# Sums of the first expert layer in two buffers, even and odd experts, the odd one added to the loaded rows by a GpSimd transfer

## The reference, cut to what matters

```python
scores = (x_flat @ Wg.T).T                       # 8 experts x 4096 tokens
top_vals, token_idx = top_k(scores, 512)         # each expert takes 512 tokens
token_w = softmax(top_vals, axis=-1)
xg = x_flat[token_idx]
h = silu(xg @ W1.T) * (xg @ W3.T)                # per expert
y = (h @ W2.T) * token_w[..., None]
out = zeros_like(x_flat).at[token_idx.reshape(-1)].add(y.reshape(-1, c))
```

## Time and profile before

| | us |
|---|---|
| median of 3 timed runs | 701.61 (701.60 to 701.68) |
| the profiled execution, its own time | 703.21 |
| the profiled execution, span from first to last instruction | 701.4 |
| busy in the span: PE, DVE, ACT, POOL | 514.5, 421.7, 343.0, 310.7 |

### The profile page before, as it was taken

One profiled execution on the slowest core, in us unless ns is written; L12 is line 12 of the kernel. 1 busy time (PEld: TensorE's weight loads), 2 busy tenths in 40 slices (PEclk: granted clock), 3 DMA queues, 4 the chain that ended last, 5 costly groups with the idle time before them and its releaser, 6 DMA issues.

```text
span 701.4 us, 13529 instructions
## 1 busy us (share of the span) xinstructions
PE 514.5 (73%) x3846; PEld 374.3 (53%) x3847; DVE 421.7 (60%) x1761; ACT 343.0 (49%) x724; POOL 310.7 (44%) x329
## 2 busy tenths in 40 slices
PE   1759521588758157878899994169999999999924
PEld 1447110356435023434334432159999999999911
DVE  4789768654312279897246878964455455545456
ACT  3815533344323034444357662246666666666525
POOL 3514300358878433342002112036676776667444
PEclk9976855599987569888899997569999999999966
DMA  7501263112333421100001010011111111111164
GB/s 187 138 0 48 79 274 147 28 41 44 42 47 39 100 100 32 32 0 1 1 1 31 16 31 21 24 22 48 46 49 45 49 49 45 49 43 52 35 230 141
DMA packets 47287, 42.22 MB, mean 60 GB/s; under 512 B 15345, under 2 KB 41322, under 8 KB 46730
## 3 DMA queue, kind: packets, MB, share of 16 engines
q1 hardware_dynamic: 31658, 25.35, 11.3%
q0 software_dynamic: 10368, 15.82, 10.1%
q10 hardware_dynamic: 5216, 0.52, 0.5%
HBM read 26.23 MB, written 15.30 MB: 59 GB/s over the span
## 4 chain that ended last, share of the span: by engine, by line
PE 48%; DVE 26%; issue 10%; POOL 6%; ACT 6%; DMA 3%; ACTq 1%; DVEq 0%; POOLq 0%; SPq 0%
PE bank L1916 18%; PE banks L1937 4%; PE bank L1937 4%; POOL sum_dram L683 3%; DVE st L1284 3%; PE bank L1774 3%; PE bank L1764 2%; PE bank L1729 2%; POOL arena L667 2%; DVE mv L1289 2%; DVE st L1014 2%; ACT arena L938 1%; POOL rstd L700 1%; PE bank L1830 1%; DVE hit L1147 1%
## 5 line engine op out<-in xcount | busy, mean ns | idle before, releaser
L1916 PE MATMUL bank<-arena 128*128 128x128 f32 x1136 | 140.9, 278 | 0.4 <-ACT arena L989 0.4
L1916 PEld LDWEIGHTS bank<-arena 128*128 128x128 f32 x1136 | 134.7, 195 | 0.7 <-ACT arena L989 0.7
L700 POOL TENSOR_TENSOR rstd<-ve,mhalf 128x4 f32<-128x4 f32 x40 | 48.8, 1219 | 167.6 <-DVE ve L1292 119.4
L1546 DVE TENSOR_TENSOR arena<-arena,bank 128x512 f32<-128x512 f32 x71 | 48.8, 688 | 82.4 <-PE bank L1916 82.4
L754 POOL DMA_INDIRECT y_dram<-arena,sidx x71 | 69.9, 985 | 44.9 <-DVE arena L1551 41.3
L975 ACT ACTIVATE arena<-wgu 128x1024 f32 x71 | 74.9, 1057 | 26.8 <-PE bank L1916 26.4
L746 POOL DMA_INDIRECT arena<-x3row_dram,gidx x71 | 68.8, 969 | 36.4 <-issue 21.0
L981 ACT ACTIVATE arena<-bank 128x512 f32<-128x512 f32 x71 | 42.4, 597 | 43.0 <-PE bank L1916 43.0
L667 POOL DMA_INDIRECT arena<-x1row_dram,idx x32 | 31.3, 979 | 43.8 <-DVE idx L1244 34.3
L683 POOL DMA_INDIRECT sum_dram<-arena,idx x28 | 44.2, 1577 | 10.9 <-issue 7.9
L1265 DVE TENSOR_TENSOR arena<-arena,bank 128x256 f32<-128x256 f32 x32 | 13.5, 422 | 57.3 <-ACT arena L870 57.3
(11 more groups left out here) (370 smaller groups left out, 1077.0 us busy)
## 6 DMA issues: line engine op xcount, KB each, us to landing
wgu<-in_wgu SPq DMA_DIRECT2D x1, 4096.0 KB, 12.4
wgu<-y_dram SPq DMA_DIRECT2D x8, 512.0 KB, 7.2
X<-in_x SPq DMA_DIRECT2D x8, 256.0 KB, 6.4
sum_dram<-zero POOLq DMA_DIRECT2D x8, 256.0 KB, 4.2
x1row_dram<-row SPq DMA_DIRECT2D x8, 256.0 KB, 2.4
w<-in_w SPq DMA_DIRECT2D x1, 2048.0 KB, 17.3
acc<-sum_dram SPq DMA_DIRECT2D x8, 256.0 KB, 2.9
w<-in_wd SPq DMA_DIRECT2D x1, 2048.0 KB, 9.9
```

The lines of the kernel that those rows point to most:

```text
L700: nc.gpsimd.tensor_tensor(out, ve[:, u], mhalf[:, 0:J], ALU.pow).then_inc(done, 1)
L1546: nc.vector.tensor_tensor(gl[:, m.pair], sgl[:, m.pair], bank[3 + m.pair][:], ALU.mult).then_inc(f_gated, 1)
L1916: last = nc.tensor.matmul(bank[first + m.pair][:, h * P:(h + 1) * P], wnow[:, m.pair, at_:at_ + P], xrT[:, m.ring], start=True, stop=True)
```

## The change

`odd_dram` is a second sum tensor. Experts 0, 2, 4, 6 go to `sum_dram`, experts 1, 3, 5, 7 to `odd_dram`. Expert 1 is a plain write now, as expert 0 is. The adds of expert e wait for those of expert e - 2, and the adds of expert 7 also for all of the even ones. `odd_dram` is cleared by eight transfers that SP issues behind the constants. SP loads a group from `sum_dram` once the even experts are done, and the load of `wd` waits for the odd ones. Then POOL issues, for each of the eight groups, a transfer from `odd_dram` into `acc` that adds to the loaded rows, and DVE waits for that transfer instead of for SP's load. In POOL's key pass it stands at the end of the step, for the group a = at(3).

```diff
+            sp.wait_ge(s_fill, LEAD + 2)
+            for t in range(T // 4):
+                sp.dma_start(odd_dram.rearrange("(t k p) d -> t p k d", p=P, k=4)[t], zero[:]).then_inc(s_later, 16)
...
-            for k in range(4):
-                sp.wait_ge(c_acc[k], 16 * E0)
+            for k in range(2):
+                sp.wait_ge(c_acc[0][k], ADDED)
...
                     if early(g, 2) and g.b:
+                        for k in range(2):
+                            sp.wait_ge(c_acc[1][k], ADDED)
                         sp.dma_start(wd, inp["wd"]).then_inc(s_w1, 16)
...
             def add0(e, ks=range(4)):
-                if e > 0:
-
-                    for k in range(4):
-                        pool.wait_ge(c_acc[k], 16 * e)
+                for k in range(2):
+                    if e == E0 - 1:
+                        pool.wait_ge(c_acc[0][k], ADDED)
+                    if e > 1:
+                        pool.wait_ge(c_acc[e % 2][k], 32 * (e // 2))
...
+                    elif e == 1:
+                        nc.gpsimd.indirect_dma_start(odd_dram, at, yw[:, n % 8], None).then_inc(c_acc[1][k % 2], 16)
+                    elif e % 2 == 0:
+                        nc.gpsimd.indirect_dma_start(sum_dram, at, yw[:, n % 8], None, compute_op=ALU.add).then_inc(c_acc[0][k % 2], 16)
                     else:
-                        nc.gpsimd.indirect_dma_start(sum_dram, at, yw[:, n % 8], None, compute_op=ALU.add).then_inc(c_acc[k], 16)
+                        nc.gpsimd.indirect_dma_start(odd_dram, at, yw[:, n % 8], None, compute_op=ALU.add).then_inc(c_acc[1][k % 2], 16)
...
+            for k in range(2):
+                pool.wait_ge(c_acc[1][k], ADDED)
+
             def key_pass(at):
-                h, g, m, l = at(2), at(1), at(0), at(-1)
+                a, h, g, m, l = at(3), at(2), at(1), at(0), at(-1)
...
                 if m:
                     logits_of_x2(m, slice(0, 3), d_lgx)
-            groups(pool, key_pass, 2, 1, 2)
+                if a:
+                    pool.wait_ge(d_acc[a.b], LEAD + 16 * a.trip + 16)
+                    nc.gpsimd.dma_start(acc[:, a.b], odd_l[ds(a.place, 1)].rearrange("o p j d -> (o p) j d"),
+                                        accum_op=ALU.add).then_inc(d_odd[a.b], 16)
+            groups(pool, key_pass, 3, 1, 2)
...
-                        dve.wait_ge(c_acc[o.ring], 16 * (o.lap - 1))
+                        dve.wait_ge(c_acc[o.lap % 2][o.ring % 2], 32 * (o.lap // 2))
...
-                    dve.wait_ge(d_acc[h.b], LEAD + 16 * h.trip + 16)
+                    dve.wait_ge(d_odd[h.b], ADDED + 16 * h.trip + 16)
```

More of the change, by code:

```diff
@@ L57 @@
 BY_DVE = 4
+ADDED = 32 * E0 // 2
 class Tally:
@@ L104, in program @@
         sum_dram = nc.dram_tensor("sum_dram", [T * P, D], F32, kind="Internal").ap()
+        odd_dram = nc.dram_tensor("odd_dram", [T * P, D], F32, kind="Internal").ap()
         x3row_dram = nc.dram_tensor("x3row_dram", [T * P, D + 2], F32, kind="Internal").ap()
@@ L413, in program @@
         c_yw = sem("c_yw")
-        c_acc = [sw_sem(f"c_added_{k}") for k in range(4)]
+        c_acc = [[sw_sem(f"c_added_{of}_{k}") for k in range(2)] for of in ("even", "odd")]
+        d_odd = c_acc[0]
         s_pch = sem("pool_chain")
@@ L647, in _ @@
             pool.wait_ge(c_zst, 16 * T // 4)
+            pool.wait_ge(s_later, LEAD + 16 * (len(LATER) + T // 4))
             pc = Tally(pool, s_pch)
@@ L680, in add0 @@
                     if e == 0:
-                        nc.gpsimd.indirect_dma_start(sum_dram, at, yw[:, n % 8], None).then_inc(c_acc[k], 16)
+                        nc.gpsimd.indirect_dma_start(sum_dram, at, yw[:, n % 8], None).then_inc(c_acc[0][k % 2], 16)
+                    elif e == 1:
+                        nc.gpsimd.indirect_dma_start(odd_dram, at, yw[:, n % 8], None).then_inc(c_acc[1][k % 2], 16)
+                    elif e % 2 == 0:
+                        nc.gpsimd.indirect_dma_start(sum_dram, at, yw[:, n % 8], None, compute_op=ALU.add).then_inc(c_acc[0][k % 2], 16)
                     else:
-                        nc.gpsimd.indirect_dma_start(sum_dram, at, yw[:, n % 8], None, compute_op=ALU.add).then_inc(c_acc[k], 16)
+                        nc.gpsimd.indirect_dma_start(odd_dram, at, yw[:, n % 8], None, compute_op=ALU.add).then_inc(c_acc[1][k % 2], 16)
             gather0(0)
@@ L708, in logits_of_x2 @@
                     ALU.mult).then_inc(d_lgx, 1)
+            odd_l = odd_dram.rearrange("(g j p) d -> g p j d", j=J, p=P)
+            for k in range(2):
+                pool.wait_ge(c_acc[1][k], ADDED)
             def key_pass(at):
-                h, g, m, l = at(2), at(1), at(0), at(-1)
+                a, h, g, m, l = at(3), at(2), at(1), at(0), at(-1)
                 if l:
@@ L1120, in _ @@
             ch.end(1)
-            dve.wait_ge(s_later, LEAD + 16 * len(LATER))
+            dve.wait_ge(s_later, LEAD + 16 * (len(LATER) + T // 4))
             total = (bank[7], bank[2])
@@ L1653, in _ @@
                 scores(c)
-            pe.wait_ge(s_later, LEAD + 16 * len(LATER))
+            pe.wait_ge(s_later, LEAD + 16 * (len(LATER) + T // 4))
             def start_total(r):
```

## The result

The changed kernel takes 707.94 us (median of 10 runs, 703.56 to 709.81); the kernel before takes 701.74 in its 10 runs (701.11 to 705.18). The ratio is 1.0072, with a 95% interval of 1.0049 to 1.0096: slower by 0.5 to 1.0%. The profiled execution took 708.23, and its span is 706.4.

A forecast was written before the change was run, and what follows sets the result against it. POOL's adds and gathers bound the first expert layer, then a landing-to-ACT chain at its end. With 1.7 gained included, ACT's start moves +3.0 (704.6), or +7.9 with the wd collision: 709.5 on a 701.61 median; range 702.8 to 712.5.

The forecast's parts named there:

- The sum: Start of key pass: ACT starts at 242.8 + R0 + R1, against 249.84 before; with collision +7.9, time 709.5.
- R0: Group 0's adding transfer, POOL's issue to landing: 5.0 if sharing freely with wd, about 9.9 if held until wd is done.
- R1: Group 1's adding transfer, POOL's issue to landing: taken as 5.0, range 4 to 6.6.
- the 2.93: Start of key pass: group 0's statistics and power, 2.63, plus POOL's gap 0.30, before group 1's transfer is issued.
- The collision with `wd`: End of expert layer: wd, released by the same landing, holds the first adding transfer; ACT 7.9 later, 709.5, chance 0.50.
- the 9.9: wd's time from issue to landing in the profile before, used as the first adding transfer's time under collision.
- the rows at the tail of `wd`: Profile before: a load of sums issued inside wd took 4.8 instead of 2.7; taken to speak for the collision.
- The price of adding: Adding transfer of 256 KB: 3.9 if the extra is paid once, 6.6 if per row; taken as 5.0.
- Expert 1's gain: POOL in first expert layer: plain writes save 2.3 in all; tile 7 cuts this to 1.7, lasting to the last landing.
- The wait at expert 7: Before expert 7's first add, POOL waits for expert 6's landing; the wait stays under the change, costed at nothing.
- The later groups: Key pass from the third group: adding transfers hidden by 0.3 at 5.0; at 6.6 they cost some 3 in all.
- The clearing: Start of kernel: SP's 2 MB clearing of odd_dram takes some 8 us, ends before 45, costs nothing.

The follow-up runs named there:

- wd_late: Changed kernel, but SP loads wd only after all eight loads of sums and all adding transfers have landed: 702.88 us, 1.0021 of before.
- both_first: Changed kernel, but POOL issues the adding transfers for groups 0 and 1 together, ahead of group 0's power: 707.30 us, 1.0073 of before.
- wd_mid: Changed kernel, but SP issues wd once the first adding transfer has landed, so it runs beside the second: 706.62 us, 1.0087 of before.
- late_nowait: Changed kernel with wd after the adding transfers, the first two of those issued together, and expert 7's wait for even experts dropped: 699.46 us, 0.9974 of before.
- late_first: Changed kernel with wd after the adding transfers and those for groups 0 and 1 issued together: 702.40 us, 1.0007 of before.

## Why the prediction was right

- **The sum.** ACT's start was to be 242.8 + R0 + R1. With the measured 9.32 and 4.41 (254.94 - 250.53) that is 256.5, and the row says 256.52. The chain was the right one, but that the sum meets to 0.02 is luck: POOL issues the first transfer at 238.61, 0.3 later than forecast, and group 1's transfer 2.60 after group 0's landing, 0.3 sooner than the 2.93. wd_late moved R0, both_first the wait for the second transfer, and wd_mid moved the collision from R0 to R1.
- **The collision with `wd`,** the forecast: R0 of 9.9, measured 9.32. wd_late takes it away, and wd_mid carries most of it to the second transfer. The mechanism was right, and the closeness of the number is in part luck: the 9.9 was the time of `wd` behind two loads of sums, with the transfer landing together with it. Not behind them, `wd` took 8.1, and the transfer landed 1.3 behind it. The large load and POOL's queue share the engines, but not freely; the rows at the tail of `wd`, from one queue, pointed the right way for two.
- **The price of adding** was mis-sized. I took 5.0 between 3.9 (the extra paid once) and 6.6 (per row); it is 4.4, near the first. 0.6 of the miss is here and 0.6 in R0, so the forecast of +7.9 at ACT's start was 1.2 too much against 6.7.
- **What is left between 6.7 and the ratio's 5.1** (interval 3.4 to 6.7) I can't settle. In the profiled pair the closing stage gave 1.6 back. The ratio of 1.0072 makes 5.1 us, while the two medians lie 6.2 apart, and the changed kernel's ten runs reach from 703.56 to 709.81, so part of it may be their scatter. The other kernels of the table come out on either side of their shift by up to 1.2, the changed one by 1.7.
- **Expert 1's gain:** 1.7 forecast, 1.73 at the gather (1.57 from the layer's first gather); of it 1.4 had reached the last landing, 1.3 from the first gather. **The wait at expert 7** stayed with the same 2.6, although the adds go to different tensors; late_nowait shows it was worth 2.2 (from the first gather to the issue of the first adding transfer it is 104.2, and 106.4 in late_first) and that nothing needed it. This I had costed at nothing, rightly for the change; but in this wait lay what two buffers could give.
- **The later groups** hid their transfers as forecast, with 5.5 to 7.3 from issue to DVE's row for a landing of 4.4 to 4.6.
- **The clearing** I costed at nothing. The profiles agree that nothing waited for it; the timed runs leave up to 2 us open.
- **The Trainium skill,** "DMA: Bandwidth & Descriptors", section "SWDGE vs HWDGE vs iDMA", says that the engine takes turns between the queues of the two kinds. The traces agree in part: POOL's packets do pass beside the 16 KB ones, 36 beside 51 from 243 to 245, but none beside 50 in the 2 us before, so turns alone don't account for all of the delay. The 2.6 that the fit of the same page, section "Anatomy of one DMA", gives as an estimate for 256 KB on POOL's path is too low here: 3.3 without adding, 4.4 with it.

## What to carry to other kernels

A transfer that moves from a load's queue to another one also loses its place ahead of whatever the load's queue holds next. When a big load is released by the same event as a small transfer on the path, order them by a wait. That was worth 4.9 of the 6.8 us at ACT's start here, and 3.6 of 5.1 by the ratios, and the big load wasn't needed for another 230 (ACT's first row behind the wait for it starts at 469.3). Splitting the sum in two paid here, by 0.1 to 0.4%, only once the wait between the two halves was dropped as well and the merging transfers were issued before anything that waits for their results.

## What the runs showed of the hardware

A direct adding transfer of 256 KB from DRAM into SBUF takes 1.32 of POOL's time and 4.4 to its landing; the plain one takes 0.80 and 3.3. Beside a load of 2 MB in 16 KB packets from SP's queue it takes 8.2 to 9.6, while that load itself takes 8.0 to 8.4 and hardly suffers: without an adding transfer beside it, it takes 7.5 to 7.7. With the load in eight issues of 2 KB packets the adding transfer takes 7.9.
